# Second cross attention: turning moved one tile and values two tiles behind the softmax, four probability buffers, row sums by VectorE, 3-bit unpacking moved to another stage

## The reference, cut to what matters

```python
scores = einsum('bqhgd,bkhd->bhgqk', q, k) * HEAD_DIM ** -0.5
attn = softmax(scores, axis=-1)
out = einsum('bhgqk,bkhd->bqhgd', attn, v).reshape(b, s, EMBED)
return out @ Wo
```

```python
q = unpack_3bit(packed)             # 8 values of 3 bits from 3 bytes
w = (q / 7.0) * (2.0 * n) - n       # one norm n for each 32 values
return einsum('bsi,oi->bso', x, w) + bias
```

## Time and profile before

| what | value |
|---|---|
| runs | 2604.83, 2596.24 and 2604.72 us, median 2604.72 us |
| the profiled execution | 2602.49 us, of which the span is 2600.7 us |
| PE, DVE, ACT, POOL busy | 95%, 50%, 36%, 28% of the span |
| mean granted TensorE clock | 0.972 |
| `l1x` from its first to its last tile | about 2336 to 2550 us of the span |
| `unpack` | 282.10 to 301.5 us of the span |

### The profile page before, as it was taken

The page is one execution under the profiler, slowest core; times in us unless marked ns, Lnnn a source line. Parts: engine busy times, 40 slices in busy tenths (PEclk is TensorE's granted clock), DMA queues, the critical chain, the costliest instruction groups (busy, mean ns, idle before and its releaser), DMA issues.

```text
span 2600.7 us, 39557 instructions
## 1 busy us (share of the span) xinstructions
PE 2468.8 (95%) x13371; PEld 2095.8 (81%) x13371; DVE 1311.8 (50%) x2997; ACT 934.3 (36%) x2495; POOL 731.0 (28%) x434
## 2 busy tenths in 40 slices
PE   5999799999999999977799999999999999989997
PEld 3788698888888898866688888888888888876665
DVE  6444744444444444464544444444444444467664
ACT  2111244444444444440233333333333333345672
POOL 4245423222222223221211111121112211226670
PEclk9999799999999999988899999999999999997998
DMA  3110212111211112101111111111111111100000
GB/s 111 57 44 29 89 59 71 48 65 48 75 54 63 50 52 77 48 25 43 41 41 44 42 42 42 42 42 42 42 42 42 42 42 42 59 1 1 1 1 33
DMA packets 36976, 119.49 MB, mean 46 GB/s; under 512 B 4920, under 2 KB 7352, under 8 KB 36928
## 3 DMA queue, kind: packets, MB, share of 16 engines
q1 hardware_dynamic: 36928, 118.88, 13.3%
HBM read 116.76 MB, written 2.10 MB: 46 GB/s over the span
## 4 chain that ended last, share of the span: by engine, by line
PE 86%; DVE 7%; issue 3%; POOL 2%; ACT 2%; SPq 0%; DMA 0%; POOLq 0%; DVEq 0%; ACTq 0%
PE pj L522 18%; PE pj L523 18%; PE pj L524 18%; PE ou L522 7%; PE ou L524 6%; PE ou L523 6%; PE pv L767 2%; PE sc L758 2%; PE pv L672 2%; PE sc L656 2%; DVE probs L1250 1%; PE tp L663 1%; PE tp L873 1%; POOL w_lo L394 1%; POOL probs L505 1%
## 5 line engine op out<-in xcount | busy, mean ns | idle before, releaser
L386 POOL TENSOR_TENSOR w_lo<-raw,w_hi 128x1024 fp32r<-128x1024 f32 x144 | 343.9, 2388 | 1453.3 <-ACT w_hi L966 1453.3
L522 PE MATMUL pj<-xt_hi,w_hi 128*128 128x512 f32 (+2 forms) x1296 | 520.3, 401 | 7.6 <-POOL w_lo L394 2.2
L523 PE MATMUL pj<-xt_lo,w_hi 128*128 128x512 f32 (+2 forms) x1296 | 502.7, 388 | 0.0
L524 PE MATMUL pj<-xt_hi,w_lo 128*128 128x512 f32 (+2 forms) x1296 | 502.2, 388 | 0.0
L522 PEld LDWEIGHTS pj<-xt_hi,w_hi 128*128 128x128 f32 x1296 | 247.2, 191 | 54.2 <-issue 6.2
L522 PE MATMUL ou<-w_hi,act_hi 128*128 128x512 f32 x684 | 275.8, 403 | 11.3 <-DVE act_lo L1488 4.8
L524 PEld LDWEIGHTS pj<-xt_hi,w_lo 128*128 128x128 f32 x1296 | 245.6, 190 | 50.1
L523 PEld LDWEIGHTS pj<-xt_lo,w_hi 128*128 128x128 f32 x1296 | 247.1, 191 | 41.9
L1209 DVE TENSOR_TENSOR x<-x,ou 128x512 f32<-128x512 f32 (+1 forms) x200 | 136.4, 685 | 285.8 <-PE ou L524 285.8
L524 PE MATMUL ou<-w_hi,act_lo 128*128 128x512 f32 x684 | 268.9, 393 | 0.0
L523 PE MATMUL ou<-w_lo,act_hi 128*128 128x512 f32 x684 | 268.1, 392 | 0.0
(11 more groups left out here) (247 smaller groups left out, 4915.5 us busy)
## 6 DMA issues: line engine op xcount, KB each, us to landing
raw<-in_l1a_w SPq DMA_DIRECT2D x80, 512.0 KB, 4.4
raw<-in_l0x_w SPq DMA_DIRECT2D x64, 512.0 KB, 3.8
side<-in_side SPq DMA_DIRECT2D x32, 512.0 KB, 4.0
raw<-in_ffn_w SPq DMA_DIRECT2D x15, 512.0 KB, 3.3
raw<-in_l1x_w SPq DMA_DIRECT2D x7, 512.0 KB, 3.7
raw<-in_l0f_w SPq DMA_DIRECT2D x6, 512.0 KB, 4.1
raw<-in_taylor_w SPq DMA_DIRECT2D x5, 512.0 KB, 6.6
x<-in_x SPq DMA_DIRECT2D x2, 1024.0 KB, 6.9
```

The lines of the kernel that those rows point to most:

```text
L386: pool.tensor_tensor(WL[:, s, :], RAW[:, s, :], f32(WH[:, s, :]), ALU.subtract).then_inc(w_ready[s], 1)
L522: pe.matmul(out, wh, xh, start=first, stop=False)
L523: pe.matmul(out, wh, xl, start=False, stop=False)
L524: return pe.matmul(out, wl, xh, start=False, stop=last)
```

## The change

In `l1x` the pipeline gets one tile deeper. Step m on PE is now `scores(m + 2)`, `transposes(m - 1)`, `values(m - 2)`. `probs` and `row_recip` get four buffers. The exponentials no longer accumulate. A `tensor_reduce` on DVE adds up the rows of `probs` in SBUF instead (`row_recip`). The factor of the scores moves into the queries, and the reduction negates its result itself, so the scaling on line 1611 is gone. The extra steps move by one. `unpack` is cut into `widen` and eight `unpack(v)`, which DVE does in the F steps 0 to 8 of the last half of `l1a`.

```diff
-        PR = sb("probs", [P, 2, 512])
+        QI = sb("q3_int", [P, 4, 64, 3], I32)
+        PR = sb("probs", [P, 4, 512])
...
                 for m in range(16):
                     if not (last and m >= 14):
                         scores(m + 2)
-                    transposes(m)
                     if not (first and m == 0):
-                        values(m - 1)
-                    if m == 3 and not first:
+                        transposes(m - 1)
+                    if not (first and m < 2):
+                        values(m - 2)
+                    if m == 4 and not first:
                         output(-1)
-                    if m == 11:
+                    if m == 12:
...
                 if last:
+                    transposes(15)
+                    values(14)
                     values(15)
                     output(1)
...
-                        done = act.activation(PR[:, bank, h * S:(h + 1) * S], sc[bank][:, h * S:(h + 1) * S], ACT.Exp,
-                                              bias=NM[:, bank, h:h + 1], scale=HD ** -0.5,
-                                              accum_out=SUMS[:, at:at + 1])
+                        done = act.activation(PR[:, m % 4, h * S:(h + 1) * S], sc[bank][:, h * S:(h + 1) * S], ACT.Exp,
+                                              bias=NM[:, bank, h:h + 1])
...
-                    dve.tensor_reduce(MX[:, bank, :], sc[bank][:].rearrange("p (h s) -> p h s", h=GQ),
-                                      axis=AX.X, op=ALU.max).then_inc(lx_max, 1)
-                    dve.wait_ge(lx_max, i * 16 + (m + 1))
-                    dve.tensor_scalar(NM[:, bank, :], MX[:, bank, :], -HD ** -0.5, None, ALU.mult).then_inc(lx_nm, 1)
+                    dve.tensor_reduce(NM[:, bank, :], sc[bank][:].rearrange("p (h s) -> p h s", h=GQ),
+                                      axis=AX.X, op=ALU.max, negate=True).then_inc(lx_nm, 1)
...
-                    dve.reciprocal(RC[:, at], SUMS[:, at]).then_inc(lx_rc, 1)
+                    dve.tensor_reduce(SUMS[:, at], PR[:, m % 4, :].rearrange("p (h s) -> p h s", h=GQ),
+                                      axis=AX.X, op=ALU.add).then_inc(lx_sum, 1)
+                    dve.wait_ge(lx_sum, i * 16 + (m + 1))
+                    dve.reciprocal(RC[:, m % 4 * GQ:(m % 4 + 1) * GQ], SUMS[:, at]).then_inc(lx_rc, 1)
...
                     row_recip(m)
-                    if not (first and m == 0):
-                        turned_lo(m - 1)
+                    if not (first and m < 2):
+                        turned_lo(m - 2)
...
                     if first and m in (5, 7, 9, 12):
                         dequantise((5, 7, 9, 12).index(m))
-                    if m == 5 and not first:
+                    if m == 6 and not first:
                         add(-1)
-                    if m == 13:
+                    if m == 14:
                         add(0)
...
             layer_norm(1)
-            unpack()
...
+                        if isinstance(i, int) and i == HG - 1:
+                            if n == 0:
+                                widen()
+                            elif n < 9:
+                                unpack(n - 1)
```

More of the change, by code:

```diff
@@ L185, in build @@
         SM = sb("row_sum_min", [P, 2])
-        RC = sb("row_recip", [P, 8])
+        RC = sb("row_recip", [P, 4 * GQ])
         KEYS = sb("lora_keys", [P, E])
@@ L872, in transposes @@
                     for h in range(GQ):
-                        done = pe.transpose(tp[:, h * S:(h + 1) * S], PR[:, bank, h * S:(h + 1) * S], IDN[:])
+                        done = pe.transpose(tp[:, h * S:(h + 1) * S], PR[:, m % 4, h * S:(h + 1) * S], IDN[:])
                     done.then_inc(tp_full, 1)
@@ L1170, in pair @@
                 for m in range(16):
-                    n, bank = nth(TP["l1x"], i, 16, m)
                     if not (last and m == 15):
                         exps(m + 1)
-                    if m == 0 and not first:
+                    if not (first and m == 0):
+                        turned_hi(m - 1)
+                    if m == 1 and not first:
                         queries(3)
-                    if m in (10, 12, 14) and not last:
-                        queries(KC + (m - 10) // 2)
-                    act.wait_ge(tp_full, n + 1)
-                    act.wait_ge(pv_full, i * 16 + (PV["l1x"] + m - 1))
-                    act.activation(AH[:, PT1 + bank * 512:PT1 + (bank + 1) * 512], tp[:], ACT.Copy).then_inc(pt_hi, 1)
-                    if m == 1 and not first:
+                    if m in (11, 13, 15) and not last:
+                        queries(KC + (m - 11) // 2)
+                    if m == 2 and not first:
                         heads(-1)
-                    if m == 9:
+                    if m == 10:
                         heads(0)
                 if last:
+                    turned_hi(15)
                     heads(1)
@@ new lines, in _, with widen @@
+            SHR, SHL, AND, OR = ALU.logical_shift_right, ALU.logical_shift_left, ALU.bitwise_and, ALU.bitwise_or
+            FIELDS = [((0, 0, 7),), ((0, 3, 7),), ((0, 6, 3), (1, 1, 2)), ((1, 1, 7),), ((1, 4, 7),),
+                      ((1, 7, 1), (2, 3, 1)), ((2, 2, 7),), ((2, 5, 7),)]
+            FIELD_END = [1 + sum(2 if len(f) == 1 else 4 for f in FIELDS[:v]) for v in range(9)]
+            def widen():
+                dve.tensor_copy(QI[:], Q3[:].bitcast(U8).rearrange("p o (n k) -> p o n k", k=3)).then_inc(dq, 1)
+                norm = QN[:].rearrange("p o g -> p (o g)")
+                dve.tensor_tensor(QN2[:], norm, norm, ALU.add)
@@ L1644, in pair @@
                     row_recip(m)
-                    if not (first and m == 0):
-                        turned_lo(m - 1)
-                    if m == 0 and not first:
+                    if not (first and m < 2):
+                        turned_lo(m - 2)
+                    if m == 1 and not first:
                         queries(3)
-                    if m in (10, 12, 14) and not last:
-                        queries(KC + (m - 10) // 2)
-                    if m == 2 and not first:
+                    if m in (11, 13, 15) and not last:
+                        queries(KC + (m - 11) // 2)
+                    if m == 3 and not first:
                         heads(-1)
-                    if m == 10:
+                    if m == 11:
                         heads(0)
```

57 lines of the change are left out of this document (27 added, 30 removed).

## The result

The changed kernel takes 2612.21 us (median of 8 runs) against 2603.45 us for the kernel before in the same sessions. The ratio is 1.0035, with a 95% interval of 1.0026 to 1.0045, so it is 9 us slower. 2602 was forecast. The profiled execution took 2612.85 us, 2611.1 of it the span, at a mean granted clock of 0.972.

What follows compares the result with a forecast made beforehand. TensorE was taken to set `l1x`'s time, losing some to waits and clock. `l1x` -2.1, unpacking out of `l0x` -6.4 and into `l1a` +8.5 summed to 0.0 on the profiled 2602.49 us, so 2602; range 2588 to 2615.

Steps and rivals of the forecast that it cites:

- DVE's extra steps: Middle pairs of `l1x`: extra work beyond some 0.3 us free is paid unless TensorE has an extra too; 49.6 us a pair.
- 0.2 for heads and queries together: Middle pair of `l1x`: the low parts of heads and queries on DVE add only 0.2 us to TensorE's time.
- slower: the clock: Rival, chance 0.09: `l1x` feeds TensorE more thinly, three tiles at half rate cost about 1.5 us each; 2616 us.
- Plain tiles: Tiles of `l1x` without extra steps: POOL's keys behind its product hold `scores`, so the period is 2.41 us.
- First and last pair: Ends of `l1x`: the first pair gains about 1.5 us, the last pair's final `values` starts 2.6 us later.
- The rival of 2648: Rival, chance 0.05: DVE's row sum waits for POOL, up to 1.0 us longer per tile, 45 us in all.
- Unpacking out of `l0x`: First cross attention: the 3.41 us pause and 3.0 us lost to the clock behind it come back, -6.4 us.
- Unpacking into `l1a`: Last half of `l1a`: unpacking on DVE delays TensorE, 6.8 us plus 1.7 for a clock dip, +8.5; bounds 3.0 to 12.
- The double field's term: Field 2 after F step 3 in `l1a`: POOL holds its OR, so step O starts 2.9 us late.
- The widening and field 0: Start of the unpacking in `l1a`: 1.1 us shows from the widening, 0.9 from field 0's cast meeting POOL.
- fields 5 to 7: F6 to F9 in `l1a`: more DVE work ahead of the values V waits for; V comes 1.9 us later.
- faster: the deeper pipeline really frees TensorE: Rival, chance 0.20: `l1x` comes down to 2.2 us a tile, waits of 20 us go; 2579 us, or 2590 with half.

Runs made afterwards that it cites:

- softmax alone: Changed kernel with the unpacking put back in the first cross attention, so only the second cross attention's change remains: 2615.4 us, ratio 1.0056 to the kernel before.
- queries first: Changed kernel with ScalarE's high part of the next queries ahead of its turning of the step's tile: 2599.7 us, ratio 0.9999 to the kernel before.
- three orders together: Changed kernel with queries' high part ahead of ScalarE's turning, low part ahead of row sum, keys ahead of scaling: 2587.9 us, 0.9957 of the kernel before.
- keys and the low part first: Changed kernel with VectorE's low part ahead of the row sum and POOL's next keys ahead of the scaling: 2597.8 us, 0.9978 of the kernel before.
- kernels with one edit each: Kernel before with only the unpacking moved, 2597.4 us (0.9981); changed kernel with the unpacking put back, 2615.4 us (1.0056).
- ScalarE's sums and the queries first: Changed kernel with row sums from ScalarE's accumulators and the queries' high part ahead of ScalarE's turning: 2583.6 us, 0.9939 of the kernel before.

## Why the forecast was wrong, step by step

- **The step that failed: "DVE's extra steps".** It laid out a middle pair at 49.6 us, a gain of 1.6 on before. A pair took 57.9, or 54.0 at full clock (softmax alone). Two things in the layout were wrong. It put "0.2 for heads and queries together" on the waits and took queries at their 0.35 us on VectorE. In the trace four of the six waits of a middle pair follow queries, 1.65, 1.06, 0.46 and 0.57 us, since the low part of the queries holds VectorE until ScalarE has turned this step's tile. The diff shows the queries moved behind `turned_hi`, and the forecast did not follow that queue. It also let `add(0)` be covered by the queries of step 13; it cost 1.17 us there, as `add(-1)` did (1.1 was forecast). In all the forecast put 3.5 us on a pair's waits (1.1, 0.2 and 2.2); the trace has 6.1 for the low part and 0.5 for the keys. The queries first (9 us) shows that the queries' place is a cause, and the three orders together (20 us) that the orders hold more than the whole loss of 9. What `add(0)` costs was not tried by itself.
- **The clock.** The forecast kept `l1x` at its clock of before. Each middle pair ran at 0.91, which took about 4 us, 8 in the two; one of them had lost 2 us to the clock before, so 6 are new. This was the rival "slower: the clock", priced at 1.5 us a tile for three tiles in the whole stage, 4.5 in all. What makes the dips is not shown. The kernels with about 3 us idle or less had none in their middle pairs. But the same code had a pair without a dip (softmax alone), and in the kernel with the keys and the low part first one pair dipped and the other didn't, with 4.1 us idle in each.
- **Plain tiles were better than forecast.** 2.41 us was forecast, bound by the keys. They took 2.17 to 2.22 (2474.62 to 2476.82 to 2479.03, for two of them). The steps of the chain were right: maximum at 1.00, row sum at 1.61, reciprocal 2.32, low part 2.41 from `scores`. The turning then came at 3.13, not 3.34. The keys held TensorE twice in a pair, not every second tile. "The prediction is wrong if the plain period falls to 2.2" came true, but the time went up: the plain steps were not where it was decided.
- **First and last pair.** -0.7 where -1.5 was forecast; +2.6 where +2.6 was. The second is luck in part: the same code took 6.7 us more than before from there to the end in the trace of the softmax alone, with a clock of 0.89 over the first 45 us where the changed kernel had 0.96.
- **Row sum and POOL.** The 64 row sums took 0.669 to 0.686 us, and none was held up by POOL. The rival of 2648 fell by that. The Trainium skill says that a `tensor_reduce` never contends with GpSimd on trn2 ("SBUF — State Buffer", "Who interferes with whom"), and this trace agrees. The Trainium skill also calls `tensor_reduce` the slowest DVE operation ("VectorE: DVE Perf Modes", "Rules for kernel authors"). Here it took no longer than the `tensor_tensor` of the same 512 elements (0.66 to 0.69).
- **Unpacking out of `l0x`.** -6.4 forecast, 6.4 us in the trace (31.3 to 24.8 us from 294.76 and 292.72 on), with pause and clock both as described. The same two codes in the kernels with one edit each give 31.2 and 24.8. The other 2.0 us of the lead of 8.5 came earlier, in code that is the same.
- **Unpacking into `l1a`.** +8.5 forecast, near the middle of its bounds; 3.6 in the trace. The double field's term was right in kind and place (2.9 forecast, 2.13 measured). The widening and field 0, 2.0 together, cost 0.2 to 0.3, fields 5 to 7 about 1 and not 1.9, and the second clock dip did not come (1.00 over 2262 to 2272). Between the two stages 1.9 us of the lead went, in code that is the same, about what had come ahead of `l0x`. Two traces of the same code differ by as much: the kernel with the softmax alone reached the values of `l0x` at 324.11, 1.9 us ahead of before, and `l1x` 1.4 behind it. Alone, the move gives 5 us (1.6 to 8.3 by its interval).

So two errors of opposite sign lay in the sum, `l1x` (-2.1 forecast, 13.3 measured) and the unpacking (+2.1 forecast, -2.8 measured); -6.4, +3.6 and +13.3 make 10.5, and the spans of the two traces differ by 10.4. The way into `l0x` was right in mechanism and size, that into `l1a` in mechanism. The rival "faster: the deeper pipeline really frees TensorE" was right about the room that is there. It needs the queries first and the row sum off VectorE (47.7 us a pair), or the three orders changed together (47.9).

## What to carry to other kernels

When work moves by a step in several engines' programs, follow each new order to its end: what stands behind the waiting instruction, and whose release waits for this very step. An in-order engine that is a third idle can still be what everyone waits for, and 0.68 us a tile cost 23 us, or some 5 that the noise hides, by where it stood. A change that loses may hold a gain: undo its parts one at a time before dropping it, and try coupled orders together too, since one of them alone can make things worse.

## What the runs showed of the hardware

- VectorE's OR, with two inputs from SBUF, ended 0.3 us after the POOL operation that it met in two of two cases: it took 2.50 us beside one of 2.44, 2.64 beside one of 2.40, and 0.42 free of POOL. None of the 64 reductions of the changed kernel was stretched (0.669 to 0.686 us).
- The granted clock differs between executions of one kernel and moves the time with it. Twelve timed executions of the kernel with the queries first go from 2586.6 us at 0.980 to 2601.9 at 0.971, and those of the kernel before from 2595.0 at 0.976 to 2604.9 at 0.972. Two more stand far off, at a far lower clock: 4110.0 us at 0.558 with the queries first, and 2615.3 at 0.916 with ScalarE's sums and the queries first, whose others took 2582.4 to 2585.6. So a difference of some 10 us between two single executions tells nothing here, and two traces can differ by 2 us or more in a stage whose code is the same.
- A middle pair of one code, with 5.3 and 5.2 us idle, took 51.9 us at a granted clock of 1.00 and 56.3 at 0.91 within one execution.
